# Inverse stage of a Fourier block: spectra loaded five steps ahead of use, results stored one image per transfer from 128 partitions

## The reference, cut to what matters

```python
for l in range(4):
    xf  = rfft2(h)
    top = einsum('bixy,ioxy->boxy', xf[:, :, :16, :16], w1[l])     # mixed spectra
    bot = einsum('bixy,ioxy->boxy', xf[:, :, -16:, :16], w2[l])
    sc  = irfft2(of)                       # of: zeros with top and bot put in
    y   = sc + einsum('bihw,oi->bohw', h, pw_w[l]) + pw_b[l]
    h   = gelu(batchnorm(y) * gamma[l] + beta[l])
```

## Time and profile before

| | us |
|---|---|
| median of 3 runs (lowest, highest) | 3170.56 (3169.16, 3171.28) |
| profiled execution | 3177.74 |
| its span | 3175.6 |
| PE, DVE, ACT busy | 2511.6, 1576.0, 1567.9 |
| four inverse stages, from the first load of spectra to the first issue of the next stage | 250.6, 314.3, 316.9, 316.7 |

### The profile page before, as it was taken

The page is one execution under the profiler, slowest core; times in us unless marked ns, Lnnn a source line. Parts: engine busy times, 40 slices in busy tenths (PEclk is TensorE's granted clock), DMA queues, the critical chain, the costliest instruction groups (busy, mean ns, idle before and its releaser), DMA issues. The chain is left out here.

```text
span 3175.6 us, 75376 instructions
## 1 busy us (share of the span) xinstructions
PE 2511.6 (79%) x32251; PEld 1645.9 (52%) x32251; DVE 1576.0 (50%) x2552; ACT 1567.9 (49%) x2659; POOL 191.7 (6%) x237
## 2 busy tenths in 40 slices
PE   6668879967777799667778987777879757784899
PEld 4655546656454466655455657544522246652344
DVE  3146667722455677235556752455510186655343
ACT  1213347722454676234456752344579747761333
POOL 0000000000000000000000000000000033220443
PEclk9779989988888899878888998888889979996999
DMA  8947789866888997778889967788875300001442
GB/s 247 245 118 181 187 246 324 289 150 185 243 253 243 299 317 237 178 201 247 240 243 305 323 206 179 216 242 242 249 229 178 94 1 1 1 1 25 97 92 62
DMA packets 243690, 604.34 MB, mean 190 GB/s; under 512 B 28415, under 2 KB 108991, under 8 KB 241087
## 3 DMA queue, kind: packets, MB, share of 16 engines
q1 hardware_dynamic: 243359, 599.51, 64.7%
HBM read 396.12 MB, written 203.93 MB: 189 GB/s over the span
## 5 line engine op out<-in xcount | busy, mean ns | idle before, releaser
L618 ACT ACTIVATE work<-P,small 128x512 f32<-128x512 f32 x512 | 323.7, 683 | 617.4 <-PE P L491 614.5
L384 PE MATMUL P<-cst,work 128*128 128x128 f32 (+1 forms) x3760 | 549.2, 286 | 56.1 <-ACT work L636 21.8
L384 PEld LDWEIGHTS P<-cst,work 128*128 128x128 f32 (+1 forms) x3760 | 412.2, 144 | 213.6 <-issue 166.6
L472 PE MATMUL P<-cst,work 64*64 64x64 f32 x8192 | 192.9, 260 | 261.0 <-DMA work<-G_d 252.6
L491 PEld LDWEIGHTS P<-cst,ATs 64*128 64x128 f32 x4096 | 267.7, 200 | 241.0 <-issue 132.9
L439 PE MATMUL P<-W,work 128*64 128x64 f32 x4096 | 282.3, 307 | 131.5 <-ACT work L589 131.1
L753 DVE COPY work<-P 128x512 f32<-128x512 f32 x256 | 175.0, 686 | 360.4 <-PE P L472 360.4
L439 PEld LDWEIGHTS P<-W,work 128*64 128x64 f32 x4096 | 280.7, 238 | 134.0 <-issue 97.1
L760 DVE BATCH_NORM_STATS2 W<-work 128x6 f32<-128x512 f32 x512 | 326.9, 680 | 9.7 <-ACT work L618 9.5
L472 PEld LDWEIGHTS P<-cst,work 64*64 64x64 f32 x8192 | 172.5, 170 | 287.0 <-DMA work<-G_d 224.1
L491 PE MATMUL P<-cst,ATs 64*128 64x128 f32 x4096 | 318.0, 298 | 0.0
(11 more groups left out here) (166 smaller groups left out, 2864.6 us busy)
## 6 DMA issues: line engine op xcount, KB each, us to landing
work<-z_d SPq DMA_DIRECT2D x384, 512.0 KB, 6.1
z_d<-work SPq DMA_DIRECT2D x256, 512.0 KB, 6.1
W<-in_wmix SPq DMA_DIRECT2D x96, 512.0 KB, 6.7
X_d<-work SPq DMA_DIRECT2D x128, 256.0 KB, 5.0
work<-X_d SPq DMA_DIRECT2D x32, 1024.0 KB, 12.5
G_d<-work SPq DMA_DIRECT2D x128, 256.0 KB, 3.3
work<-G_d SPq DMA_DIRECT2D x256, 128.0 KB, 5.0
hz<-z_d SPq DMA_DIRECT2D x64, 512.0 KB, 4.6
```

The source lines that it names most:

```text
L384: return nc.tensor.matmul(out, in_, ident[0:n, 0:n], start=True, stop=True, is_transpose=True)
L472: last = nc.tensor.matmul(P[v][g * 64:g * 64 + 64, m * 64:m * 64 + 64], Gt[a.par][o, x:x + 64], i1c[o, k:k + 64], start=True, stop=True)
L618: nc.scalar.activation(ychunk(a, h), P[4 + 2 * (a.q % 2) + h][:, :], ACT.Identity, bias=bias0 if first else pwb_c).then_inc(S["eY"], 1)
```

## The change

The mixed spectra of pair p are loaded at SP step 4p-4 (with the pair before), not 4p; those of pairs 0 and 1 both at step 0. The wait on `pI1` is that of the pair whose buffer is filled. The stores of a half of `ybuf` are still two of 512 KB, at the same steps, with the same semaphore; each now takes one image h from all 128 partitions (both g), where before it took both images from 64 partitions. The destination `z_y[t, u, h, k]` has the dimensions g (2, 2048 elements apart), o (64, 4096 apart) and n (1024); before, `z_y[t, u, g, k]` had o (64), h (2) and n (1024).

```diff
-        z_y = z_d.rearrange("(t u) (h o) (g k n) -> t u g k o h n", u=2, h=2, g=2, k=2)
+        z_y = z_d.rearrange("(t u) (h o) (g k n) -> t u h k g o n", u=2, h=2, g=2, k=2)
...
+                def load_mixed(n):
+                    for v in range(2):
+                        for h in range(2):
+                            sp.dma_start(Gt[n.par][v * 64:v * 64 + 64, h * 512:h * 512 + 512], G_s[h, n.t, n.par, v]).then_inc(gl[n.par], 16)
+                load_mixed(At(0, 0, 0, 0))
+
                 def step(t, u, q):
                     a = At(t, u, q, 0)
-                    if q == 0 and a.ok:
-                        wait(sp, "pI1", l * 32 + a.pair * 2 - 2)
-                        for v in range(2):
-                            for h in range(2):
-                                sp.dma_start(Gt[u][v * 64:v * 64 + 64, h * 512:h * 512 + 512], G_s[h, a.t, u, v]).then_inc(gl[u], 16)
+                    n = At(t, u, q, -4)
+                    if q == 0 and n.ok:
+                        wait(sp, "pI1", l * 32 + n.pair * 2 - 2)
+                        load_mixed(n)
                     b = At(t, u, q, 8)
                     if b.ok and b.q % 2 == 1:
 
                         sp.wait_ge(S["eY"], l * 128 + b.s * 2 + 2)
-                        for g in range(2):
-                            sp.dma_start(z_y[b.t, b.par, g, b.q // 2], ybuf[b.q // 2][g * 64:g * 64 + 64, :].rearrange("p (h n) -> p h n", h=2)).then_inc(yst[b.q // 2], 16)
+                        for h in range(2):
+                            sp.dma_start(z_y[b.t, b.par, h, b.q // 2], ybuf[b.q // 2][:, h * 1024:h * 1024 + 1024]).then_inc(yst[b.q // 2], 16)
```

## The result

| | before | after |
|---|---|---|
| median, us | 3170.92 | 4929.12 |
| profiled span, us | 3175.6 | 4930.2 |
| four inverse stages, first load of spectra to next stage, us | 250.6, 314.3, 316.9, 316.7 | 698.1, 748.9, 750.3, 755.8 |
| everything else, us | 1977.1 | 1977.1 |

The kernel is slower by a factor of 1.553 (95% interval 1.550 to 1.557). The forecast was 5100 us with a range of 4850 to 5800. All of the added time lies in the inverse stages, 2953.1 us against 1198.5; the rest is the same to 0.1 us.

What follows compares the result with a forecast made beforehand. Two DMA engines full of stores were to bound the kernel at 49 us a pair; inverse stages of 742 + 3 x 795 = 3127 us against 1198.5 add 1928 to the profiled 3177.7, so 5100 us, range 4850 to 5800.

Steps and rivals of the forecast that it cites:

- What bounds now: Inverse stages before the change: a late spectra load sets the 19.3 us pair; engines need 12.7 us, the DMA queue 16.7.
- Two engines: New stores: destination's outermost dimension g has 2 entries, so each store runs on two DMA engines, taken as always the same.
- Price of a packet: Stores on two engines: a 4 KB packet costs 165 ns, so a pair's stores need 42.2 us of each engine.
- My lower bound: Store packet of 4 KB: at least 155 ns, estimated from the load's 165; it gives 4929 us in total.
- The line through the two rows of lone packets: Store packet price: a line through 384 B (23 ns) and 2 KB (87 ns without completion) gives 166 ns for 4 KB.
- The queue is never empty: Inverse stages: the other half's stores last 24 us, covering the 6 us until SP stores again.
- Early spectra at zero: Spectra loaded four steps earlier: the gain of 4.5 us a pair is worth nothing under a 49 us period.
- The sum: Inverse stages: 742 us for the first layer and 795 for each other, 3127 in all against 1198.5, adding 1928 us.
- First rival (all 16 engines): Stores split by their 128 source partitions run on 16 engines at the load's rate: 2870 us; chance 0.07.
- different engines for each store: Rival on the stores: two engines, but different ones each time, 22 us a pair, 3300 us; chance 0.05.
- dearer packets: Rival: a packet on a lone engine costs 190 to 220 ns, or the queue runs dry: 5550 to 6080 us; chance 0.12.
- What would show it: Signs in the new profile: 2 completions a store, DMA share about a quarter, store landing over 20 us, pair 49 us.

Runs made afterwards that it cites:

- the runs with 4, 8, 16 and 128: Changed kernel with the stores' destination given outermost dimension 4, 8, 16 or 128, rows landing elsewhere in z_d: 3683, 3170, 2943 and 2920 us.

## Why the prediction was right, point by point

- **What bounds now.** That a late load sets the period was right: moving it alone gave 194 to 205 us. Its 12.7 us of work and 4.5 us of standing come to 17.2, though, not 19.3: the 2.1 us between them, which the prediction passes over, are matmuls at the lower clock behind the wait. That the DMA engines "stand close behind" was right too, but at 14.5 us a pair and not 16.7, since busy time of the queue shrank once it ran without gaps.
- **Two engines.** Right, and the step on which all hung. The 3584 missing completion packets, the share of 12.7% in a stretch of stores alone, and the completions and times of the runs with 4, 8, 16 and 128 show it. That they are the same two each time, which I had taken without a row, is shown by the pair's time: 45.5 us are what all 256 store packets of a pair need on one engine, with its share of the loads; spread over changing engines they would have given some 22 us.
- **Price of a packet.** This is the term that was mis-sized: 154 to 156 ns (by the period, by the window) against 165. At 17.7 us for each nanosecond that is 159 to 195 us, and the sum (5106) lies 174 us above the profiled execution of the changed kernel (4932.35). So the price accounts for the gap. My lower bound, 155 ns, gave 4929. Luck had a part in the 165. The line through the two rows of lone packets took 23 ns off for a completion, whose record lasts 9 ns; with 9, the same line gives some 196 ns, and the sum would have come to some 5650 us. What a lone packet of 2 KB takes (some 106 ns by its record) is more than one in the stream of the changed kernel (median 84), so such packets were the wrong rows to draw the line through. The lower bound of 155 ns, estimated from the loads, was the good one.
- **The queue is never empty.** Right: never fewer than two packets are under way. The period is 45.5 us where 49 were forecast, by the price of the packet.
- **Early spectra at zero.** Right here (ratios 1.555 and 1.553), though the move is worth some 200 us in every version whose stores use 16 engines and whose matmuls are as here.
- **The sum.** First layer 742 forecast, 698.1 measured; the others 795 each, 748.9 to 755.8.
- **First rival (all 16 engines).** It did not come, and its price was too low: 2870 forecast, 2920 measured with 16 engines, since packets cost 198 ns there in mixed traffic and not 165. For the same reason the break-even is at 8 engines (3170 us) and not at 7, which was not run. The other rivals are excluded: different engines for each store by the 45.5 us of a pair, dearer packets by the 154 to 156 ns.
- **What would show it.** DMA share "about a quarter": 0.29. Other stages unchanged: yes. ACT waits on the stores: as far as the code tells what the name "issue" stands for. The landing of a store, forecast at over 20 us, is in no view of the changed kernel.

## What to carry to other kernels

Before a store is widened to more partitions, write down the outermost dimension of both sides as the transfer will carry it: if two of the DRAM dimensions can't be merged, the outer one may be 2, and the transfer runs on two engines, as here. Its small packets in the trace tell the number: data rows plus one completion for each engine. A mean DMA share of 0.3 with all engines idle was here the sign of two full ones. A wait of 960 us can cost next to nothing while a longer one covers it, and one that is not covered can cost more than its length, here 4.5 us and 2.3 more in matmuls at the lower clock.

## What the runs showed of the hardware that I had not expected

- Mixed loads and stores of 4 KB rows on 16 engines ended at 318 to 328 GB/s with the share at 1.01, for stores from 64 partitions as well as from 128. Alone, stores from 64 partitions reached 197 to 205 GB/s and loads onto 128 reached 405; beside loads, storing from 128 partitions gained only 57 us in 2977.
- The time that a full engine needs for a 4 KB packet rose with the number of engines that carry stores: 154, 155, 171 and 198 to 206 ns on 2, 4, 8 and 16.
- Behind a wait of 4.49 us PE ran some 5 us at a granted clock of 0.53, and its matmuls took 1.5 to 1.8 times as long.
- Stores of the same bytes in smaller pieces that change the partition half were faster, not slower: 2954 against 2977 us. That stores from the two halves overlap better is my guess; no run tests it apart from the size.
